# One weight scale taken two units earlier, two weight conversions reordered, in a macaron block

## The reference, cut to what matters

```python
x = x + 0.5 * ffn(layernorm(x))          # x: 8 x 1024 x 128
x = x + linear_attention(layernorm(x))   # 16 heads of 8
x = x + 0.5 * ffn(layernorm(x))

def ffn(x):                              # 8 experts, all of them for every token
    for wg, wu, wd in experts:           # 128x512, 128x512, 512x128, float32
        acc += (silu(x @ wg) * (x @ wu)) @ wd
```

## Time and profile before

| | |
|---|---|
| median of 3 runs | 2056.73 us (2056.58 to 2057.06) |
| profiled execution | span 2054.4 us from first to last instruction; its own device time is not given, and the span is 2.3 us under the median |
| PE busy | 2047.3 us (100%), 9514 matmuls |
| DVE, ACT, POOL busy | 1662.1 us (81%), 1439.1 us (70%), 694.2 us (34%) |
| granted TensorE clock | 1.000 over the span |
| chain that ended last | 97% PE |

### The profile page before, as it was taken

One profiled execution on the slowest core, in us unless ns is written; L12 is line 12 of the kernel. 1 busy time (PEld: TensorE's weight loads), 2 busy tenths in 40 slices (PEclk: granted clock), 3 DMA queues, 4 the chain that ended last, 5 costly groups with the idle time before them and its releaser, 6 DMA issues.

```text
span 2054.4 us, 29536 instructions
## 1 busy us (share of the span) xinstructions
PE 2047.3 (100%) x9514; PEld 933.1 (45%) x9514; DVE 1662.1 (81%) x2734; ACT 1439.1 (70%) x2511; POOL 694.2 (34%) x706
## 2 busy tenths in 40 slices
PE   9999999999999999999999999999999999999999
PEld 5444444444444444444444444444444444444444
DVE  8887787888887878788888787978787878877776
ACT  7877767766776676677766776676677766666665
POOL 6511134334423432345244323442344244410000
PEclk9999999999999999999999999999999999999999
DMA  7111256244733542555245335453454346421100
GB/s 215 16 22 20 62 109 127 59 96 88 144 81 79 116 88 73 86 122 117 66 96 116 78 77 102 92 106 89 84 124 102 93 87 136 83 36 21 21 11 16
DMA packets 242571, 172.58 MB, mean 84 GB/s; under 512 B 157424, under 2 KB 212720, under 8 KB 242416
## 3 DMA queue, kind: packets, MB, share of 16 engines
q1 hardware_dynamic: 208480, 128.48, 26.3%
q0 software_dynamic: 33936, 42.21, 12.7%
HBM read 99.09 MB, written 30.15 MB: 63 GB/s over the span
## 4 chain that ended last, share of the span: by engine, by line
PE 97%; DVE 1%; DMA 1%; issue 1%; ACT 0%; POOL 0%; SPq 0%; DVEq 0%; ACTq 0%; POOLq 0%
PE bank L670 11%; PE bank L649 11%; PE bank L666 11%; PE bank L667 11%; PE bank L630 11%; PE bank L637 10%; PE bank L631 10%; PE bank L653 10%; PE bank L650 10%; DMA xn<-half_tok 1%; PE bank L676 0%; PE bank L675 0%; PE bank L674 0%; DVE bank L970 0%; DMA arena<-in_L_ffn_Wu 0%
## 5 line engine op out<-in xcount | busy, mean ns | idle before, releaser
L768 ACT ACTIVATE silu_sb<-bank,scal 128x512 f32<-128x512 f32 x1024 | 704.4, 688 | 575.8 <-PE bank L637 568.5
L970 DVE SCALAR_TENSOR_TENSOR bank<-silu_sb,scal,bank 128x512 f32<-128x512 f32 x984 | 737.4, 749 | 371.3 <-ACT silu_sb L768 367.7
L977 DVE TENSOR_TENSOR h_lo<-bank,h_hi 128x512 f16<-128x512 f32 x984 | 673.4, 684 | 0.1
L775 ACT ACTIVATE h_hi<-bank 128x512 f16<-128x512 f32 x984 | 581.8, 591 | 4.0 <-DVE bank L970 3.9
L630 PE MATMUL bank<-xn,wg_hi 128*128 128x512 f16 x1024 | 388.1, 379 | 0.5 <-ACT wg_hi L758 0.4
L670 PE MATMUL bank<-h_hi,wd_lo 128*128 128x512 f16 x1024 | 388.1, 379 | 0.4 <-DVE wd_lo L958 0.4
L649 PE MATMUL bank<-xn,wu_hi 128*128 128x512 f16 x1024 | 388.2, 379 | 0.2
L666 PE MATMUL bank<-h_hi,wd_hi 128*128 128x512 f16 x1024 | 388.1, 379 | 0.2 <-ACT down_sb L783 0.2
L650 PE MATMUL bank<-xn,wu_hi 128*128 128x512 f16 x1024 | 388.1, 379 | 0.0
L653 PE MATMUL bank<-xn,wu_lo 128*128 128x512 f16 x1024 | 388.1, 379 | 0.0
L667 PE MATMUL bank<-h_lo,wd_hi 128*128 128x512 f16 x1024 | 388.1, 379 | 0.0
(11 more groups left out here) (144 smaller groups left out, 1367.5 us busy)
## 6 DMA issues: line engine op xcount, KB each, us to landing
arena<-rep_scratch SPq DMA_DIRECT2D x128, 512.0 KB, 6.9
arena<-arena POOLq DMA_DIRECT2D x56, 512.0 KB, 4.9
turn_scratch<-turn_sb SPq DMA_DIRECT2D x196, 64.0 KB, 1.9
x_tok<-turn_scratch POOLq DMA_DIRECT2D x49, 256.0 KB, 5.1
rep_scratch<-arena SPq DMA_DIRECT2D x16, 512.0 KB, 2.7
x_tok<-in_L_attn_x SPq DMA_DIRECT2D x16, 256.0 KB, 5.4
term_scratch<-arena SPq DMA_DIRECT2D x8, 512.0 KB, 3.3
arena<-term_scratch SPq DMA_DIRECT2D x8, 512.0 KB, 4.4
```

The costliest lines, as they stand in the source:

```text
L768: act.activation(silu_sb[:, n % 3, :], gate_ps[n % NG][:, :], ACT.Silu, scale=unscale[G[group(n)]]).then_inc(sem("silu"), 1)
L970: dve.scalar_tensor_tensor(up_ps[n % NUP][:, :] if n >= NF else h_sb(n), silu_sb[:, n % 3, :], (h_scale if n >= N_ALL else h_first)[group(n)],
L977: dve.tensor_tensor(h_lo[:, n % NH, :], up_ps[n % NUP][:, :], h_hi[:, n % NH, :], ALU.subtract).then_inc(sem("h_lo"), 1)
```

## The change

Four entries of the tables move. The down scale of experts 2 to 7 is taken by DVE in unit 14 instead of 16, and PE does its spread in unit 14 instead of 16. The diagonal that the spread reads stays in unit 13. Expert 2's down weights are converted by ACT in unit 15 instead of 17 and by DVE in unit 15 instead of 18. Expert 3's up weights are converted by ACT and POOL in unit 17 instead of 15.

```diff
-              (11, "w_max", (2, 2)), ..., (13, "w_diag", 3), (16, "w_scale", 3),
+              (11, "w_max", (2, 2)), ..., (13, "w_diag", 3), (14, "w_scale", 3),
-    SPREADS = [(1, 1), (11, 2), (16, 3)]
+    SPREADS = [(1, 1), (11, 2), (14, 3)]
-    LATE = {..., ("g", 3): 14, ("u", 3): 15, ("d", 2): 17}
+    LATE = {..., ("g", 3): 14, ("u", 3): 17, ("d", 2): 15}
-    VECTOR_LOW.update({("g", 2): 13, ("d", 2): 18, ("d", 0): 2})
+    VECTOR_LOW.update({("g", 2): 13, ("d", 2): 15, ("d", 0): 2})
```

More of the change, by code:

```diff
@@ L61, in macaron_program @@
               (7, "w_max", (1, 1)), (8, "w_max", (1, 2)), (9, "w_max", (1, 3)), (9, "w_diag", 2), (10, "w_max", (2, 1)),
-              (11, "w_max", (2, 2)), (12, "w_scale", 2), (12, "w_max", (2, 3)), (13, "w_diag", 3), (16, "w_scale", 3),
+              (11, "w_max", (2, 2)), (12, "w_scale", 2), (12, "w_max", (2, 3)), (13, "w_diag", 3), (14, "w_scale", 3),
               (24, "h_scales", 0)]
     WARM = (22, 4, 9)
-    SPREADS = [(1, 1), (11, 2), (16, 3)]
-    LATE = {("g", 1): 0, ("u", 1): 1, ("d", 0): 2, ("d", 1): 6, ("g", 2): 12, ("u", 2): 13, ("g", 3): 14, ("u", 3): 15, ("d", 2): 17}
+    SPREADS = [(1, 1), (11, 2), (14, 3)]
+    LATE = {("g", 1): 0, ("u", 1): 1, ("d", 0): 2, ("d", 1): 6, ("g", 2): 12, ("u", 2): 13, ("g", 3): 14, ("u", 3): 17, ("d", 2): 15}
     VECTOR_LOW = {(w, x): 4 * x + 8 + v for w, v in (("g", -5), ("u", -4), ("d", 1)) for x in range(4 - (w == "d"), X)}
-    VECTOR_LOW.update({("g", 2): 13, ("d", 2): 18, ("d", 0): 2})
+    VECTOR_LOW.update({("g", 2): 13, ("d", 2): 15, ("d", 0): 2})
     order = [(1, 0), (1, 1), (1, 2), (1, 3), (2, 0), (1, 4), (2, 1), (1, 5), (2, 2), (1, 6), (1, 7)]
```

## The result

The changed kernel takes 2060.80 us (median of 13 runs, 2058.39 to 2062.70) against 2056.49 us of the kernel before (13 runs, 2055.69 to 2057.06). The ratio is 1.0021, 95% interval 1.0014 to 1.0028: slower by 4.3 us or 0.2%, and the interval leaves no doubt of the sign. The time lies in the predicted range, 1.3 us over the point. The profiled run took 2060.16 us and has a span of 2058.2 us.

What follows compares the result with a forecast made beforehand. PE was taken as the bound, so lost time stays: 3.62 us wait plus 0.10 bare weight load minus 0.91 won in unit 21 gives +2.81, on 2056.73 that is 2059.5 us, range 2058.3 to 2061.2.

Steps and rivals of the forecast that it cites:

- PE is the bound and a delay in unit 14 stays: Whole kernel: PE idles only 0.26 us from 56 to 2000 us, so earlier lost time is not made up.
- The wait for the diagonal: Unit 14: PE stands still from 41.30 to 44.92 until DVE's diagonal is ready, 3.62 us.
- 6.33 busy us: DVE from 38.36 to 44.86: busy 6.33 of 6.50 us, read as working through a backlog, not waiting for PE.
- The bare weight load, 0.10: Unit 14: a spread that comes out of a wait starts with its weight load bare, adding 0.10 us.
- The 0.91 us of unit 21: Unit 21, first down product with expert 2: waits of 0.38 (bank evacuation) and 0.53 us (`wd_lo`) vanish, -0.91 us.
- `wd_lo` and what is behind it: DVE's moved conversion ends between 49.5 and 52.5, well before PE needs it; operations queued behind it cost nothing.
- The bounds by the port rule: DVE and POOL ports lock to whoever starts first; the start order at 42.05 decides between +2.81 and +1.95 us.
- the low bound of +1.95: Unit 14: if DVE got in before POOL, the diagonal would be there 0.86 us sooner, the sum +1.95 us.
- The sum: Units 14 to 21: 3.62 + 0.10 - 0.91 = +2.81 us, giving 2059.5 us.
- The chance of the clock falling: Rival: the idle wait in unit 14 lowers PE's clock, together +4.3 to +4.8, 2061.0 to 2061.5 us; chance 0.13.
- the line of 4.1 us: Whole kernel: changes within 0.2%, 4.1 us, can't be told from none; within 0.86, slower 0.13, faster 0.01.
- The second place: Behind 56 us: PE has only 0.26 us of idle time, so at best 2059.2; under 2058 had chance 0.02.

Runs made afterwards that it cites:

- diag12: Changed kernel with the down scale's diagonal on DVE at the end of unit 12 instead of 13; 2056.53 us against 2056.31 for the kernel before.
- longer: Changed kernel with one more DVE reduction over 2048 columns, result unused, ahead of unit 14's diagonal; 2064.99 us.
- scale_only: Kernel before with only the down scale and its spread moved to unit 14, all conversions in their old places; 2061.37 us.
- low17: Kernel before with only expert 2's down low half on DVE moved from unit 18 to 17; 2056.23 us against 2056.45.
- scale15: Changed kernel with scale and spread in unit 15 and expert 2's down conversions in unit 16; 2057.22 us against 2056.45 for the kernel before.
- fill_half_b: Second set of the changed kernel with 7 dummy matmuls on PE ahead of unit 14's wait, filling about 1.5 us of it; 2061.55 us.

## Why the prediction was right, and where it was not

**PE is the bound and a delay in unit 14 stays.** Shown: in the profiled run the starts of unit 21 are 2.87 us later, and nothing behind it gives that back.

**The wait for the diagonal.** Predicted 3.62 us, measured 3.60. That what stands in front of the diagonal on DVE sets it is shown by `diag12`, where taking two operations away made the wait 0.83. But the 6.33 busy us that the prediction read as DVE's own work hold time beside POOL: the diagonal takes 0.28 us with POOL idle, and here 0.99, until 0.08 us after POOL's L1142 (43.35 + 1.49 = 44.84). The kernel before has the same, 44.86 after 44.77, and `longer` too. About 0.7 us of the wait go with that POOL operation. No run moved it alone.

**The bare weight load, 0.10.** From the spread's start to the next matmul it is 0.33 us, against 0.22 for the spread in unit 16 of the kernel before (45.18 to 45.40). Right.

**The 0.91 us of unit 21.** Won, as predicted. But the prediction gave the moved conversions a part in it; `scale_only` shows that the delay does it alone.

**`wd_lo` and what is behind it.** Start expected near 48.7, measured 48.65; between the bounds at 1.14 us. No late operand of expert 3 showed up. (The 1.50 us that the prediction took for POOL's half of it is the row of expert 2; expert 3's took 1.16. The sum does not use it.)

**The bounds by the port rule.** The rule that the prediction took from the Trainium skill (SBUF — State Buffer, "SBUF: two separate sides") fits in that DVE was held while POOL worked: DVE's operation ended 0.54 to 0.56 us after the end of POOL's each time, 43.75 after 43.21 and 55.76 after 55.21, 49.79 after 49.24 in the changed kernel and 51.86 after 51.31 in `low17`. That is why it took from 1.07 to 3.76 us. But "the rows fit it" was too strong for the order of starts. The 3.76 us operation started at 52.00, 0.47 us before POOL's pair, and was held all the same. POOL was issuing a DMA just then:

```profile
51.43 1.46 POOL L1183 DMA_DIRECT2D x_tok<-turn_scratch  x1
```

Whether that row counts as the first, no run separates. No run reversed the order of the two starts at 42.05 and 42.15 either, and with a shorter `wg_lo` the diagonal would still have had POOL's L1142 beside it, so the low bound of +1.95 is not shown.

**The sum.** +2.81 predicted; 2.79 in the rows. For the runs of the changed kernel with a clock of 1.000 (7 of 24 over both sets) the median is 2059.39 us, against the 2059.5 forecast. Part of this closeness is luck: the base of 2056.73 was 0.24 us over the median of 13 runs, and the profiled run, one of the seven, holds 0.93 us that the sum does not have.

**The chance of the clock falling is the step that failed.** I gave it 0.13. A mean clock below 1.000 came in 17 of 24 runs (71%), whose median is 2061.29, 1.9 us above the others. That is the time of this rival, 2061.0 to 2061.5. Its price, 1.5 to 2 us from the start's rows, is that of the late fall (1.7), and too low for the full one (2.7 and 2.8). So the forecast time was that of the less frequent case; the median of all runs lies between, nearer to the rival, and the range held it only because it reached into that case. The measured 4.31 us also lie just over the line of 4.1 us, on the side "slower" that had 0.13. I argued with how busy PE was on both sides of the gap, and no row supported that this protects the clock. That the fall follows from the idle PE is shown by three traces with it at the wait (waits of 3.6 us in the changed kernel and in `scale_only`, of 5.8 in `longer`), by 5 of 5 runs in `longer`, and by none in the 22 filled runs and the 11 of `diag12`; that all 17 fell at this wait is likely, not shown. The Trainium skill (TensorE: Matmul & The Clock Gate, "HAM oscillation — how this bites in real kernels"), which the prediction weighed as speaking against the change, was right that such a wait can put the clock down: in the rows at 41.4 to 51 the burst behind the wait starts cold, as it says. In `scale_only` the burst started at the full clock and went cold 1 us later, and in the changed kernel's first profiled run the clock did not fall at all.

**The second place.** I had taken the 0.26 us of idle time behind 56 us as a sign of no slack either way. But operands arrive just in time at the change of blocks: the DMA took 11.9 us before and 12.8 in the changed kernel, and PE lost 0.93 us there. Of the 0.13 us idle before, 0.06 stand at this place, and the prediction read past them. Over the profiled runs the wait was 0 to 2.6 us; its cause is open.

## What to carry to other kernels

Before an instruction that waits is moved earlier on the bounding engine, lay the timeline of the engine that feeds it beside it: here the operand was ready 0.3 us before its old place and 3.6 us after its new one, and the gain behind it was 0.9. Price a single long wait on PE as the wait plus a possible stretch at half clock (1.7 or 2.7 us here), and look at each run's mean granted clock, not only at the profiled run, which may be one where it did not fall. Dummy matmuls in the wait help to tell the two prices apart, if the rest of the run stays the same. A wait that was 0.1 us in the trace can be a place where the next microsecond of DMA time counts in full.

## What the runs showed of the hardware

- With one PE wait of 3.6 us between dense matmuls the mean granted clock was below 1.000 in 17 of 24 runs (and in 10 of 11 of `scale_only`); with one of 5.8 us in 5 of 5; with dummy matmuls in it in 0 of 22; with one of 1.66 us in 0 of 11 (`scale15`), of 0.83 us in 0 of 11 (`diag12`). Of the three profiled runs with 3.6 us the clock fell to 0.50 inside the wait in one and cost 2.7 us, fell about 1 us after PE had resumed in another and cost 1.7 us, and stayed up in the third. In `longer` it fell inside the wait and cost 2.8 us.
- A 2.6 us wait for a DMA in the middle of the kernel was followed by a fall of the clock in one of two profiled runs (`fill_half_b`).
- The same DVE operation, 128x512 float32 to float16 with two SBUF inputs, took 0.74 to 3.76 us, and ended 0.54 to 0.56 us after the POOL operation beside it; the 128x128 diagonal took 0.28 us with POOL idle, and 1.00 us with a POOL operation beside it, ending 0.08 or 0.09 us after that one.
